# First stage of a four-layer graph network in column groups of 768 instead of 512, with two staged buffers and single turning banks

## The reference, cut to what matters

```python
h = relu(layernorm(x))                       # L0
e = concat(par_u[0]*par_u[1]*(diag_u[:,None]*h[:2048] @ W_u) + h[:2048],
           par_i[0]*par_i[1]*(diag_i[:,None]*h[2048:] @ W_i) + h[2048:])
g = adj @ (adj.T @ e)
x = x + layernorm(g)*gamma + beta + h
h = relu(layernorm(x)); x = x + h + ...      # L1: adj @ h
# L2: three chained products adj @ T, each folded into the output with its own 64 x 64 weights
# L3: degree = sum(adj + I, axis=1); relu(D^-1/2 (adj + I) D^-1/2 (h @ W + b))
```

## Time and profile before

| | |
|---|---|
| runs | 1675.48 us median (1671.74 to 1678.89) |
| profiled execution, its own time | 1680.66 us |
| its span | 1678.8 us |
| PE busy | 1566.2 us (93%) |
| DVE, ACT, POOL busy | 467.6, 266.1, 95.0 us |
| moved by DMA | 531.26 MB, mean 316 GB/s |
| 303 loads of turned tiles, 100 raw loads, 100 stores | 1024 KB each |

### The profile page before, as it was taken

How to read it: one execution, slowest core, us unless ns; L and a number is a source line. 1 busy time by engine, 2 the same in 40 slices (tenths; PEclk the granted TensorE clock), 3 DMA queues, 4 the chain that set the end, 5 groups by cost and what they waited for, 6 DMA issues and landing times.

```text
span 1678.8 us, 19779 instructions
## 1 busy us (share of the span) xinstructions
PE 1566.2 (93%) x8040; PEld 651.0 (39%) x8040; DVE 467.6 (28%) x643; ACT 266.1 (16%) x351; POOL 95.0 (6%) x103
## 2 busy tenths in 40 slices
PE   5888989899998999899999989999999999999788
PEld 2444434444444445433333333333333343333232
DVE  6544444444444444511111020001000031111211
ACT  2233323332333334200000000000000001000000
POOL 2300000000000003800000000000000000000000
PEclk9999999999999999999999999999999999999899
DMA  8499999999999999999887668788676748737997
GB/s 283 170 326 325 322 321 323 326 331 327 334 328 330 333 332 392 407 426 426 341 372 319 263 289 327 290 285 298 275 296 262 323 172 314 296 124 305 424 404 317
DMA packets 124218, 531.26 MB, mean 316 GB/s; under 512 B 20096, under 2 KB 21376, under 8 KB 72576
## 3 DMA queue, kind: packets, MB, share of 16 engines
q1 hardware_dynamic: 117728, 528.83, 83.9%
q10 hardware_dynamic: 6432, 1.57, 0.4%
HBM read 424.20 MB, written 106.17 MB: 316 GB/s over the span
## 4 chain that ended last, share of the span: by engine, by line
PE 69%; DMA 25%; DVE 3%; issue 1%; POOL 1%; SPq 1%; ACT 0%; DVEq 0%; ACTq 0%
PE turned L366 31%; DMA raw<-in_adj_dram 22%; PE acc L366 20%; PE turned L412 6%; PE aux L375 6%; PE aux L501 2%; DMA whole<-adj_t 1%; DMA out_dram<-sq 1%; PE turned L521 1%; DVE deg_part L667 1%; PE aux L511 1%; PE aux L503 1%; SPq L311 1%; PE aux L420 0%; PE aux L431 0%
## 5 line engine op out<-in xcount | busy, mean ns | idle before, releaser
L366 PE MATMUL turned<-whole,F 128*64 128x512 f32 x1184 | 276.3, 598 | 0.1
L570 ACT ACTIVATE whole<-turned 128x1024 f32<-128x1024 f32 x200 | 193.8, 1022 | 357.3 <-PE turned L412 357.3
L366 PE MATMUL turned<-whole,E 128*64 128x512 f32 x1064 | 249.4, 595 | 0.0
L375 PE MATMUL aux<-raw,E 128*64 128x512 f32 x800 | 194.8, 608 | 57.1 <-DMA raw<-in_adj_dram 56.6
L667 DVE TENSOR_REDUCE deg_part<-raw 128x2048 f32 (+1 forms) x100 | 227.7, 2277 | 0.0
L412 PEld LDWEIGHTS turned<-ident,raw 128*128 128x128 f32 x1600 | 173.8, 141 | 75.2 <-issue 72.7
L412 PE MATMUL turned<-ident,raw 128*128 128x128 f32 x1600 | 197.9, 276 | 0.3 <-ACT whole L570 0.3
L366 PE MATMUL acc<-whole,t_cur 128*64 128x512 f32 x800 | 193.7, 605 | 0.0
L699 DVE TENSOR_TENSOR h_acc<-acc,h_acc 128x512 f32<-128x512 f32 x90 | 62.2, 691 | 301.1 <-PE acc L366 301.1
L366 PEld LDWEIGHTS turned<-whole,F 128*64 128x64 f32 x1184 | 82.5, 137 | 156.8 <-issue 153.4
L366 PE MATMUL acc<-whole,R 128*64 128x512 f32 x560 | 129.2, 600 | 5.1 <-DVE R L660 5.1
(11 more groups left out here) (91 smaller groups left out, 548.5 us busy)
## 6 DMA issues: line engine op xcount, KB each, us to landing
whole<-adj_t SPq DMA_DIRECT2D x303, 1024.0 KB, 9.9
raw<-in_adj_dram SPq DMA_DIRECT2D x100, 1024.0 KB, 8.7
adj_t<-whole SPq DMA_DIRECT2D x100, 1024.0 KB, 9.9
out_dram<-sq ACTq DMA_DIRECT2D x10, 128.0 KB, 14.2
fold_weigh<-in_L_gnn_weights_dram ACTq DMA_DIRECT2D x2, 48.0 KB, 2.3
gam<-in_L_gnn_ln_gamma_dram ACTq DMA_DIRECT2D x1, 32.0 KB, 2.8
bet<-in_L_gnn_ln_beta_dram ACTq DMA_DIRECT2D x1, 32.0 KB, 2.9
b<-in_L_gnn_bias_dram ACTq DMA_DIRECT2D x1, 32.0 KB, 3.7
```

The costliest lines, as they stand in the source:

```text
L366: last = nc.tensor.matmul(bank[half, :], v[:, i, :], tile[:, i, :], start=start and i < 2, stop=stop and i >= SUB - 2)
L375: last = nc.tensor.matmul(aux[0][half, :], E[:, m * SUB + a, :], raw[:, m, a, :], start=(m == 0 and a < 2), stop=(m == NB - 1 and a >= SUB ...
L570: nc.scalar.activation(whole[m % STAGED][:, h * HS:(h + 1) * HS, :], turned[h][:, :, :], ACT.Copy).then_inc(half_copied, 1)
```

## The change

The first stage goes in 7 groups: six of 768 columns (6 chunks of 128) and a last one of 512 (4 chunks). A raw tile of a wide group is 1.5 MB in runs of 3 KB, a turned one 1.5 MB with 12 KB on each partition. `adj_t` is laid out (row block, partition, group, columns), so that all of a partition's turned data of a row block lie in one row of 86,016 bytes; the second stage reads its 8 KB pieces from there. There are two staged buffers of 12 KB a partition in place of five of 8 KB; the first group loop is written out for SP, and for the other engines its last two rounds are.

A turned chunk (4 transposes) goes through one of three single banks, each with its own copy by ACT of 128 x 512 and its own semaphore step. t of a wide group needs two banks (`t_acc`, 384 columns in each), so `products_for_t` makes 16 matmuls of 384 columns in place of 8 of 512 (two per product, as fp32 goes in two). The wait for `deg_summed` moves from PE (before turning) to SP (before the reload).

At the start SP issues X in three parts (2, 3 and 5 row blocks) around the first raw load; the diagonal weights are loaded as 40 rows of 128 and turned by one PE transpose and one ACT copy; the two small `par` loads go to ACT's queue. The sums of group 0 leave DVE's loop for E: four come behind it, the rest in group 0's steps. PE turns tile (0, 0) and (0, 1) within its loop, after the steps m = 7 and 9, and ACT copies them there. Of the 15 slots of the second stage two are new early ones (loaded before the last group's stores), ten lie over the raw tiles of the last group, three over the staged buffers. Some buffers share memory in new ways (`cen` in `t_t`, `S` and `ego_t` in `h_acc`).

The diff, cut, in its own order: constants and buffers, SP, PE, ACT, DVE.

```diff
+CHUNKS = 6
+GW = CHUNKS * P
+NG = -(-N // GW)
+CHUNKS_LAST = NT - (NG - 1) * CHUNKS
+TURN_BANKS = 3
+TURN_EARLY = {7: 0, 9: 1}
+SUMS_AHEAD = 4
+X_PARTS = [(0, 2), (2, 5), (5, 10)]
-STAGED = 5
-SLOTS = STAGED + NB
+STAGED = 2
+EARLY_SLOTS = 2
+LATE_SLOTS = 3
+SLOTS = EARLY_SLOTS + NB + LATE_SLOTS
...
-        adj_t = nc.dram_tensor("adj_t", (NB, NB, P, SUB, B), F32, kind="Internal").ap()
+        adj_t = nc.dram_tensor("adj_t", (NB, P, NG, CHUNKS * B), F32, kind="Internal").ap()
...
+        turned = [ctx.enter_context(nc.psum_tensor(f"turned{i}", [P, B], F32)) for i in range(TURN_BANKS)]
+        t_acc = ctx.enter_context(nc.psum_tensor("t_acc", [P, 2, B], F32))
+        t_rows = ctx.enter_context(nc.psum_tensor("t_rows", [P, B], F32))
...
+        def chunk_no(g, m, c):
+            return g * (NB * CHUNKS) + (m * chunks(g) + c)
+        def stores_before(g, m):
+            return g * (16 * NB // STAGED) + 16 * (m // STAGED)
...
+            load_x(0)
+            sp.dma_start(diag_rows[0:U // P, :], du_d.rearrange("(t p) -> t p", p=P)).then_inc(diag_in, 16)
+            sp.dma_start(diag_rows[U // P:NT, :], di_d.rearrange("(t p) -> t p", p=P)).then_inc(diag_in, 16)
+            sp.dma_start(w_in[:, 0, :], wu_d).then_inc(early_in, 16)
+            sp.dma_start(w_in[:, 1, :], wi_d).then_inc(early_in, 16)
+            load_x(1)
+            load_first(0)
+            load_x(2)
+            for m in range(1, NB):
+                load_first(m)
...
             def load_next(g, m):
-                sp.wait_ge(half_turned, g * (NB * 2) + (2 * m + 2))
+                sp.wait_ge(chunk_turned, chunk_no(g, m, chunks(g)))
+                sp.wait_ge(deg_summed, sums_to(g, m))
+                src = adj_v[:, m, :, (g + 1) * GW:(g + 1) * GW + chunks(g + 1) * P]
...
+            for n in range(EARLY_SLOTS):
+                first_load(n)
             for j in range(NB):
-                store(NB - 1, j)
-                sp.wait_ge(stored[m % STAGED], 16 * (2 * k + m // STAGED + 1))
-                load_turned(j)
+                store(NG - 1, j)
+                first_load(EARLY_SLOTS + j)
...
+            def turn_chunk(g, m, c):
+                q = chunk_no(g, m, c)
+                if not isinstance(g, int) or q >= TURN_BANKS:
+                    pe.wait_ge(chunk_copied, q - (TURN_BANKS - 1))
+                bank = turned[(m * chunks(g) + c) % TURN_BANKS]
+                for a in range(SUB):
+                    last = nc.tensor.transpose(bank[:, a * P:(a + 1) * P], raw_of(g, m)[:, a, c * P:(c + 1) * P],
+                                               ident[:, :])
+                last.then_inc(chunk_turned, 1)
...
+                if m in TURN_EARLY:
+                    for c in range(CHUNKS):
+                        turn_chunk(0, TURN_EARLY[m], c)
...
-                    if m + 1 < NB or followed:
-                        pe.wait_ge(deg_summed, g * NB + (m + 2))
-                        turn_half(g, m + 1, 0)
-                        if m == 0:
-                            turn_t(g)
-                        turn_half(g, m + 1, 1)
+                    if turns:
+                        for c in range(TURN_BANKS):
+                            turn_chunk(*following, c)
+                    if m == 0:
+                        turn_t(g)
+                    if turns:
+                        for c in range(TURN_BANKS, chunks(following[0])):
+                            turn_chunk(*following, c)
...
+            def copy_turned(g, m, some):
+                for c in some:
+                    act.wait_ge(chunk_turned, chunk_no(g, m, c + 1))
+                    if c == 0 and not (isinstance(g, int) and g * NB + m < STAGED):
+                        act.wait_ge(stored[m % STAGED], stores_before(g, m))
+                        act.wait_ge(used, g * NB + (m - STAGED + 1))
+                    nc.scalar.activation(staged_of(m)[:, c * B:(c + 1) * B], turned[(m * chunks(g) + c) % TURN_BANKS][:, :],
+                                         ACT.Copy).then_inc(chunk_copied, 1)
...
-                    if m < NB - 1:
-                        sum_rows(0, m)
+            for m in range(SUMS_AHEAD):
+                sum_rows(0, m)
```

More of the change, by code:

```diff
@@ L312, in _, with load_x @@
-            for m in range(NB):
-                sp.dma_start(raw[:, m], adj_v[:, m, :, 0, :]).then_inc(raw_in[m], 16)
-            def store(g, m):
[L316 to L320, removed]
+            def load_x(i):
+                t = slice(X_PARTS[i][0] * SUB, X_PARTS[i][1] * SUB)
+                sp.dma_start(X[:, t, :], x_v[:, t, :]).then_inc(x_in[i], 16)
@@ L361, in _, with multiply @@
         def _(pe):
-            def multiply(v, tile, bank, start, stop):
-                for i in range(SUB):
+            def multiply(v, tile, bank, start, stop, count=SUB):
+                for i in range(count):
                     half = slice((i % 2) * D, (i % 2 + 1) * D)
                     last = nc.tensor.matmul(bank[half, :], v[:, i, :], tile[:, i, :],
-                                            start=start and i < 2, stop=stop and i >= SUB - 2)
+                                            start=start and i < 2, stop=stop and i >= count - 2)
                 return last
@@ L457, in _ @@
             pe.wait_ge(e_ready, NB)
-            pe.wait_ge(deg_summed, 1)
-            for h in range(HALVES):
-                turn_half(0, 0, h)
             group(0)
-            with pe.Fori(1, NB - 1) as g:
+            with pe.Fori(1, NG - 2) as g:
                 group(g)
-            group(NB - 1, followed=False)
+            group(NG - 2)
+            group(NG - 1, followed=False)
             def features_wait(p, k):
@@ L556, in _ @@
                     copy_ego(m - 2)
+                if m - 2 in TURN_EARLY:
+                    copy_turned(0, TURN_EARLY[m - 2], range(CHUNKS))
             w123_v = w2_d[1:4].rearrange("k i o -> i k o")
@@ L562, in _ @@
                 act.dma_start(dst, src).then_inc(late_in, 16)
-            def copy_turned(g, m):
-                for h in range(HALVES):
-                    act.wait_ge(half_turned, g * (NB * 2) + (2 * m + h + 1))
-                    if h == 0 and not (isinstance(g, int) and g * NB + m < STAGED):
-                        act.wait_ge(stored[m % STAGED], g * (16 * NB // STAGED) + 16 * (m // STAGED))
-                        act.wait_ge(used, g * NB + (m - STAGED + 1))
-                    nc.scalar.activation(whole[m % STAGED][:, h * HS:(h + 1) * HS, :], turned[h][:, :, :],
-                                         ACT.Copy).then_inc(half_copied, 1)
             def copy_t(g):
@@ L576, in copy_t @@
                     act.wait_ge(t_turned, g)
-                nc.scalar.activation(t_t[:, :], aux[0][:, :], ACT.Copy).then_inc(t_copied, 1)
+                columns = chunks(g) * P // 2
+                nc.scalar.activation(t_t[:, 0:2 * columns].rearrange("p (h k) -> p h k", h=2), t_acc[:, :, 0:columns],
+                                     ACT.Copy).then_inc(t_copied, 1)
             def take_t(g):
@@ L582, in take_t @@
                     act.wait_ge(used, g * NB)
-                nc.scalar.activation(t_cur[:, :, :], aux_rows[1], ACT.Copy).then_inc(t_ready, 1)
+                rows = t_rows[:, 0:chunks(g) * D].rearrange("p (a d) -> p a d", d=D)
+                nc.scalar.activation(t_cur[:, 0:chunks(g), :], rows, ACT.Copy).then_inc(t_ready, 1)
             def end_of_layer(i):
```

212 lines of the change are left out of this document (124 added, 88 removed).

## The result

The changed kernel takes 1621.01 us (median of 4 runs, 1618.39 to 1622.31) against 1677.18 us for the kernel before beside it: ratio 0.9662, 95% interval 0.9626 to 0.9699, 56 us faster. 1635 was predicted. The profiled execution has 1620.43 us and a span of 1618.6, before 1678.8: 60.2 us less.

What follows compares the result with a forecast made beforehand. The first stage was taken as bound by DMA, closely followed by PE. Start 75, 49 wide steps 436 and group 5 78 make 589 us, 50 gained; less 7 in the last group, 43 off 1680.66: forecast 1635, range 1612 to 1674.

Steps and rivals of the forecast that it cites:

- PE sets the pace: Rival for the first stage: mixing adds nothing to longer runs, wide steps of 8.55 us, 1617 us in all; chance 0.14.
- What a run of bytes costs a DMA engine: First stage: mixing reads and writes adds 25 ns to a short run, 15 to a long one; wide step 8.9 us.
- The wide step: Groups of 768 columns: 8.9 us a step at DMA's pace, with PE's floor at 8.55 us.
- Three banks: Turning a wide tile: PE waits for copies from the fourth chunk on, some 0.3 us in six chunks.
- The start: Up to the products for the next t: E of tile 0 near 16, DMA idle 51 to 65, end near 75 us.
- The early turning gives DMA nothing; it only takes 5.7 us off PE: Start: the first reload waits for its sum anyway, so turning tiles 0 and 1 early only saves PE 5.7 us.
- Group 5: Last wide group, with narrow reloads: ten steps of 7.8 us, 78 us in all.
- A store may take 14.8 us: Two staged buffers: a store has 14.8 us to land and needs 10.8, so it fits with 4 us to spare.
- the slower rival: Staged buffers: the copy waits for the store and PE for the copy, steps of 10.1 us, 1703 us; chance 0.12.
- The last group: Narrow group: steps of 5.22 us against PE's 4.66, 5.6 us in ten, plus early loads; a loss of 7 us.
- The second stage: Untouched but for its addresses, with PE full from 720 us: change 0, bounds 0 and +8 us.
- The rival of the layout at half the rate: Second stage: loads of rows 84 KB apart at half of 426 GB/s, over 2000 us in all; chance 0.05.

Runs made afterwards that it cites:

- experiment 3: Transfers of the kernel alone, all computation left out, issued with a full queue: pairs of 2 and 8 KB runs move 413 GB/s.
- experiment 5: Transfers alone, each reload issued a fixed time after the reload two before landed: narrow pairs 6.31 us, 5.73 with store ahead; 1.5 MB pairs 7.65 and 7.69.
- experiment 6: The kernel before, with each tile's store moved from behind its own reload to just ahead of the next tile's reload: 1640.7 us, ratio 0.9789.
- Experiment 1: The changed kernel with groups of 512 columns throughout, two staged buffers and the other edits kept: 1699.3 us, ratio 1.0117 to the kernel before.
- experiment 12: The changed kernel with tiles (0, 0) and (0, 1) turned behind the first products instead of among them: 1616.3 us, ratio 0.9622 to the kernel before.
- experiments 1 and 2: Both: the changed kernel with groups of 512 columns; the first with two staged buffers, 1699.3 us, the second with five, 1699.0 us.
- 9: The changed kernel with the store of a tile just turned put ahead of the reload for the tile after next: 1622.4 us, ratio 0.9656.

## Why the prediction was right in time and wrong in its cause

The time lies in the range, and within the forecast's own 1622 to 1650 but for 1 us. The forecast's mechanism isn't what happened: the rival "PE sets the pace", given 0.14 and 1617 us, is. Its reason, that mixing adds nothing to longer runs, turned out to hold for the short ones too. That the range held is no support for the mechanism, since it reached down to PE's floor.

- **The failed step is "What a run of bytes costs a DMA engine".** It divided share times time by the number of runs and took the result, 109 ns for a mixed run of 2 KB, as the engine's price. In experiment 3 the same pairs make 413 GB/s, in experiment 5 the same bytes move at 330 GB/s or 367 by the order of issue alone, and runs of 2 and 3 KB give one pace. What held the stage was the loop of landing, PE's work and reissue, at 6.3 us, though the share showed 0.96. Hence "the first stage is bound by DMA" was wrong for the kernel before too: experiment 6 changes no byte and wins 37 us.
- **The wide step.** Predicted 8.9 us by DMA, 8.55 as PE's floor with 0.3 us between chunks. Measured 8.22 on PE, 8.45 with t's turning. In the loop's terms: PE turns and does the products between landing and reissue for 2.68 + 2.91 = 5.6 us, (5.6 + 10.3) / 2 = 8.0, just under 8.22. The width wins because a landing grows only from 8.7 to 10.3 us while a step has 1.5 times the columns, and PE's work covers it. Experiment 1 shows that the gain is the width's, 5 that transfers so paced take 6.31 us narrow and 7.65 wide, 6 that the kernel before was held by the loop. Why a landing grows by so little was not taken apart. 436 us were predicted for 49 steps, 414.0 measured.
- **Three banks.** The 0.3 us of wait a step at the fourth chunk didn't occur: it is 1.1 us in 47 tiles. A bank less costs 46 us.
- **The start.** The products for the next t end at 78.2 us, 75 predicted. E of tile 0 at 14.91 (near 16), the last E at 59.78 (its loop's end near 61), the empty DMA (52 to 60 at 0.00), the reload's wait for its sum: all as written. Missing were the wait of 3.08 us and the half clock behind it, and a landing of 10.4 us where about 6 were counted. "The early turning gives DMA nothing; it only takes 5.7 us off PE" is wrong in its second half: it delays the last E by 5.6 us and costs 3.4 us at the start (experiment 12).
- **Group 5.** 78 us predicted, 571.18 - 492.16 = 79.0 measured, near by accident: a clean step is 7.36 us (542.62 to 549.99 on ScalarE, the copies of two tiles), and t's turning, PE's waits for the copies behind late stores (2.04 us at 526.99) and the slower clock after that make up the rest. "A store may take 14.8 us" was figured for steps of 8.9 us; at 8.22 the same sum allows 13.6 (2 x 8.22 - 2.91 - 0.7 + 0.75). The median landing is 13.2 and the longest 17.9, so 20 copies began late where I wrote none. The 103.5 us beside them are the whole idle time of ScalarE before these copies and not a loss; in the wide steps a late store adds up to 0.7 us to it, in group 5 up to 2.2. Of the slower rival that much is true; its steps of 10.1 us didn't come.
- **The last group.** Predicted a loss of 7 us; measured from the group's first turning to the second stage's first product 54.5 against 46.1 before: 8.5. The steps are 4.8 to 5.1 us, where 5.22 was counted; the wait at 581.74 (3.61 us) is what the term lacked, and the products behind it took 3.43 us in place of 1.94. It laid 5.6 of the 7 us to two staged buffers in place of five; with narrow groups that exchange is worth 1.4 us (experiments 1 and 2).
- **The second stage.** 0 predicted, 0.9 us gained (992.9 us from its first product to the end against 993.8). The rival of the layout at half the rate didn't come, and no run shows a rate like that: rows 84 KB apart load at 423 GB/s against 424. The Trainium skill, DMA: Bandwidth & Descriptors, Latency and other measured facts, gives 207 GB/s at a row pitch of 512 KiB and 103 at 4 and 8 MiB. No run here has a pitch that large.
- **The sum.** 67.7 gained - 8.5 + 0.9 = 60.1 of 60.2 us; predicted 50 - 7 = 43. By its terms up to the last group: 78.2 + 414.0 + 79.0 = 571.2 against 75 + 436 + 78 = 589.

## What to carry to other kernels

A DMA share near 1 doesn't show that the transfers are the limit. Divide what a stretch moves by its time and compare with a stretch that has a full queue; if it is lower, look for a loop (landing, work, reissue), and first change what is issued right behind the late transfer. A new order must not hold up the transfer that it is to help: in experiment 6 the store put ahead was ready, the reload went out 0.6 us later and landed 1.7 us sooner, and 37 us were won. In 9 the store was not ready, the reload went out 1.2 us later, landed 0.5 us sooner and had 0.4 us to spare, and nothing was won.

Idle time that ends with a late transfer isn't what that transfer costs. Compare it with the idle time of a step in which another engine ends it: here 5.49 us against 5.25.

An early piece of work on an idle-looking engine is only free if nothing that a slower queue waits for stands behind it.

## What the runs showed of the hardware

- The same 1 MB pairs at a DMA share of 0.97 moved 330 GB/s and at 1.03 moved 413. A share of 0.97 left room for a quarter more.
- The order of issue changed both landing times: with a store of 1 MB issued 1.1 us behind a reload of 1 MB the reload landed in 8.7 us and the store in 10.0; with the store just ahead of the next reload, in 7.2 and 4.9.
- With a full queue, runs of 2 KB and 3 KB load at 388 and 403 GB/s in experiment 3, and at 409 and 401 in the two kernels (20 to 24 us); in paced pairs of 1.5 MB they give 7.69 and 7.65 us.
- After 3.08 us without work PE's granted clock was 0.50 (1.2 GHz) from 74 to 76 us, and 16 matmuls took 4.22 us in place of 2.75. After 1.94 us without work in experiment 12 they took 2.80 at a clock of 1.00. In the changed kernel a wait of 2.04 us before 526.99 was followed by 0.50 from 528 to 530 us, and 12 matmuls that take 2.79 us elsewhere took 3.54:

```profile
528.00:530.00 2.00, 2.00 (x9) 1.34 (x9) 0.00 (x0) 1.52 (x3) 0.00 (x0) 0.50 0.56 235
```
